# Transposes of a ternary feed-forward moved from TensorE to DMA, with the row rounding moved to ScalarE

## What is computed

```python
def _quant_weight(w):
    scale = jnp.mean(jnp.abs(w)) + EPS
    wq = jnp.clip(jnp.round(w / scale), -1.0, 1.0) * scale
    return w + jax.lax.stop_gradient(wq - w)

def _quant_act(x):
    scale = jnp.maximum(jnp.max(jnp.abs(x), axis=-1, keepdims=True), EPS) / 127.0
    xq = jnp.clip(jnp.round(x / scale), -128.0, 127.0) * scale
    return x + jax.lax.stop_gradient(xq - x)

def bitlinear(x, w):
    return jnp.einsum('bsi,oi->bso', _quant_act(x), _quant_weight(w))

gate = jax.nn.sigmoid(bitlinear(x, w_gate))      # 512 -> 2048
up = bitlinear(x, w_up)                          # 512 -> 2048
h = gate * up
return bitlinear(h, w_down)                      # 2048 -> 512
...
x = x + jnp.tanh(g_ffn[0]) * _L0_ffn_ref(_layernorm(x, axis=-1), L0_ffn_w_gate, L0_ffn_w_up, L0_ffn_w_down)
```

## Time and profile before

| | us |
|---|---|
| median of 3 runs | 1309.91 (1309.18 to 1309.97) |
| the profiled execution, its own time | 1311.82 |
| its span in the trace | 1310.0 |
| busy in the span: TensorE matmul | 1114.2 (85%) |
| VectorE | 1020.2 (78%) |
| ScalarE | 668.9 (51%) |
| GpSimd | 525.9 (40%) |
| all 16 DMA engines, mean share | about 31% |

### The profile page before, as it was taken

The page is one execution under the profiler, slowest core; times in us unless marked ns, Lnnn a source line. Parts: engine busy times, 40 slices in busy tenths (PEclk is TensorE's granted clock), DMA queues, the critical chain, the costliest instruction groups (busy, mean ns, idle before and its releaser), DMA issues. The chain is left out here.

```text
span 1310.0 us, 16066 instructions
## 1 busy us (share of the span) xinstructions
PE 1114.2 (85%) x4802; PEld 449.6 (34%) x4802; DVE 1020.2 (78%) x1560; ACT 668.9 (51%) x783; POOL 525.9 (40%) x403
## 2 busy tenths in 40 slices
PE   4976499999899899937999995999999998279687
PEld 2543022222222222203444442444444444134232
DVE  5677498887788788517999983688788878777888
ACT  1646047887688688844666663011000000586896
POOL 5756011535343353450101111888888784000021
PEclk9989569999899899978999997899999999589879
DMA  8799624436345354214111101111112110000011
GB/s 319 254 315 337 200 84 142 132 124 192 107 128 158 112 155 122 72 32 188 34 47 48 48 17 36 34 63 65 60 53 65 63 50 31 1 1 1 1 64 65
DMA packets 65213, 131.65 MB, mean 100 GB/s; under 512 B 13864, under 2 KB 31656, under 8 KB 61552
## 3 DMA queue, kind: packets, MB, share of 16 engines
q1 hardware_dynamic: 65152, 130.95, 30.7%
HBM read 106.53 MB, written 22.02 MB: 98 GB/s over the span
## 5 line engine op out<-in xcount | busy, mean ns | idle before, releaser
L807 DVE TENSOR_REDUCE mneg<-ps_m 128x1 f32<-128x512 f32 x512 | 319.6, 682 | 67.5 <-PE ps_m L720 55.7
L1348 PE MATMUL ps_y<-kv,toeplitz_sb 128*128 128x512 f32 x640 | 279.5, 596 | 8.6 <-POOL kv L1260 8.6
L688 ACT ACTIVATE probs<-ps_s 128x1024 f32<-128x1024 f32 x256 | 251.3, 1022 | 66.0 <-PE ps_s L742 65.0
L720 PE MATMUL ps_m<-k_stack,q_stack 112*128 112x512 bf16 x512 | 189.3, 410 | 26.9 <-DMA k_stack<-mask_k 16.1
L1348 PEld LDWEIGHTS ps_y<-kv,toeplitz_sb 128*128 128x128 f32 x640 | 121.1, 191 | 154.8 <-issue 154.8
L742 PE MATMUL ps_s<-q_stack,k_stack 112*128 112x512 bf16 x512 | 155.2, 387 | 10.4 <-ACT probs L688 10.1
L752 PE MATMUL ps_o<-probs,v_all 128*17 128x512 f32 x1024 | 136.5, 605 | 0.4 <-ACT probs L688 0.4
L1260 POOL TENSOR_TENSOR kv<-vT,ctxT_sb 128x2048 f32<-128x2048 f32 x32 | 118.8, 3711 | 39.2 <-PE ps_y L1348 32.4
L983 PE MATMUL ps_g<-w,xT_f 128*128 128x512 bf16 x512 | 119.7, 383 | 7.1 <-DVE h_f L1130 6.3
L1414 DVE TENSOR_TENSOR z<-ps_y,ctxT_sb 128x1024 f32<-128x1024 f32 x64 | 77.9, 1218 | 47.2 <-PE ps_y L1348 47.2
L1313 ACT ACTIVATE w_anchor<-w_f 128x512 f32<-128x512 f32 x32 | 20.1, 628 | 180.6 <-DMA w_f<-in_w 180.6
(11 more groups left out here) (159 smaller groups left out, 1628.1 us busy)
## 6 DMA issues: line engine op xcount, KB each, us to landing
w_sweep<-in_w SPq DMA_DIRECT2D x8, 1536.0 KB, 10.1
q_stack<-q_parts SPq DMA_DIRECT2D x96, 128.0 KB, 3.5
k_stack<-k_parts SPq DMA_DIRECT2D x96, 128.0 KB, 3.3
w_sweep<-in_w SPq DMA_DIRECT2D x16, 768.0 KB, 5.4
w_sweep<-in_w SPq DMA_DIRECT2D x16, 512.0 KB, 3.4
toeplitz_sb<-in_toeplitz SPq DMA_DIRECT2D x32, 256.0 KB, 2.6
w_f<-in_w SPq DMA_DIRECT2D x32, 256.0 KB, 2.9
k_parts<-qk_part SPq DMA_DIRECT2D x24, 256.0 KB, 6.9
```

Source lines behind the costliest of these rows:

```text
L688: nc.scalar.activation(pr[:, k % 2, 2 * slot:2 * slot + 2, :], S[:, 2 * slot:2 * slot + 2, :], ACT.Exp).then_inc(exp_done, 1)
L720: nc.tensor.matmul(M[:, bank(j), :], Q[0:ROWS, slot, hd, tc * P:(tc + 1) * P], K[0:ROWS, slot, hd, :], start=True, stop=True).then_inc(max ...
L807: nc.vector.tensor_reduce(mneg[:, h, tile % LT, tile // LT:tile // LT + 1], M[:, bank(j), :], AX.X, ALU.max, negate=True).then_inc(max_red, 1)
L1348: mm = nc.tensor.matmul(Y[:, q % 3, l2, :], T[:, g % 2, (lt - m) * P:(lt - m + 1) * P], kv[:, g % 2, m, :], start=(m == 0), stop=(m == lt))
```

## The change

The transposes leave TensorE: SyncE issues one DMA from SBUF to SBUF with `transpose=True` for each `xq_f` tile (128x512, 128 KB) and one for each `hq_f` tile (128x2048, 512 KB). The copies out of PSUM go with them. Centring and both rounding steps of the rows go from VectorE to ScalarE, as `centre` and `round_x`; for that one small operation (`nb`, 128x16) is added before the first tile. The maximum, the scales and the reciprocal stay in VectorE's `prepare`. The tile loop is written out in full. The `ctxT_sb` loads move behind the first tile's `turn_x(1)` in SyncE's queue. GpSimd's update of tile t-2 is written in the pass of tile t.

```diff
 def over_tiles(eng, n, tile):
 
-    tile(0, 0, True, False)
-    tile(1, 1, False, False)
-    with eng.Fori(1, n // 2 - 1) as i:
-        tile(2 * i, 0, False, False)
-        tile(2 * i + 1, 1, False, False)
-    tile(n - 2, 0, False, False)
-    tile(n - 1, 1, False, True)
+    for t in range(n):
+        tile(t, t % 2, t == 0, t == n - 1)
...
             @block.sync
             def _(sp):
+                def turn_x(t, par):
+
+                    sp.wait_ge(xq_ready, t + 1)
+                    if t >= 2:
+                        sp.wait_ge(gu_done, NCH * (t - 1))
+                    sp.dma_start(xT[:, par], xq[:, par, :], transpose=True).then_inc(xT_ready[par], 16)
+
+                def turn_h(t, par):
+
+                    sp.wait_ge(hq_ready, t + 1)
+                    if t >= 2:
+                        sp.wait_ge(down_done, t - 1)
+                    sp.dma_start(hT[:, par], hq[:, par, :], transpose=True).then_inc(hT_ready[par], 16)
+
                 def tile(t, par, first, last):
                     if not early(t):
                         sp.wait_ge(w8m_ready, t - 1)
                     sp.dma_start(w8c[:, par], A["w8"][bass.ds(2 * t, 2)].rearrange("m p l -> p m l"))\
                         .then_inc(w8c_loaded[par], 16)
-
-                for lt in range(LT):
-                    sp.dma_start(core.cT[:, lt], A["ctxT"][lt * P:(lt + 1) * P]).then_inc(core.cT_loaded, 16)
+                    if not last:
+                        turn_x(t + 1, 1 - par)
+                    if not first:
+                        turn_h(t - 1, 1 - par)
+                    if first:
+                        for lt in range(LT):
+                            sp.dma_start(core.cT[:, lt], A["ctxT"][lt * P:(lt + 1) * P]).then_inc(core.cT_loaded, 16)
+                    if last:
+                        turn_h(t, par)
+
+                turn_x(0, 0)
                 over_tiles(sp, ROWT, tile)
...
                 def down(t, par, first):
                     if not first:
                         pe.wait_ge(d_taken, t)
-                    for half in range(2):
-                        pe.wait_ge(hT_ready, 2 * t + half + 1)
-                        for k in range(half * KT // 2, (half + 1) * KT // 2):
-                            mm = nc.tensor.matmul(D[:], hT[:, par, k, :], wd[:, k, :], start=(k == 0),
-                                                  stop=(k == KT - 1))
+                    pe.wait_ge(hT_ready[par], 16 * (t // 2 + 1))
+                    for k in range(KT):
+                        mm = nc.tensor.matmul(D[:], hT[:, par, k, :], wd[:, k, :], start=(k == 0), stop=(k == KT - 1))
                     mm.then_inc(down_done, 1)
...
                         if c == 1 and not early(t):
                             down(t - 2, par, same(t, 2))
-                        if c == 2 and not last:
-                            turn_x(t + 1, 1 - par)
-                        if c == 3 and not first:
-                            turn_h(t - 1, 1 - par, same(t, 1))
...
             @block.scalar
             def _(act):
                 ln_scalar(core, act, 1)
...
+                act.wait_ge(xf_start, 1)
+
+                def centre(t, par):
+
+                    nc.scalar.activation(xn[:, par, :], X[:, t, :], ACT.Identity, bias=nb[:, t:t + 1],
+                                         scale=core.rstd[:, t:t + 1]).then_inc(xn_ready, 1)
+
+                def round_x(t, par):
+
+                    act.wait_ge(rx_ready, t + 1)
+                    nc.scalar.activation(xn[:, par, :], xn[:, par, :], ACT.Identity, bias=core.magic,
+                                         scale=sc[:, par, RX:RX + 1]).then_inc(xr_ready, 1)
+                    act.wait_ge(xr_ready, t + 1)
+                    if t >= 2:
+                        act.wait_ge(xT_ready[par], 16 * (t // 2))
+                    nc.scalar.activation(xq[:, par, :], xn[:, par, :], ACT.Copy, bias=-MAGIC).then_inc(xq_ready, 1)
+
+                centre(0, 0)
+                centre(1, 1)
+                round_x(0, 0)
...
                         nc.scalar.activation(sg[:, c % 2, :], G[:, c % 2, 0, :], ACT.Sigmoid,
                                              scale=sc[:, par, GS:GS + 1]).then_inc(sig_ready, 1)
+                        if c == 0 and not last:
+                            round_x(t + 1, 1 - par)
                         if c == 1 and not first:
                             round_h(t - 1, 1 - par)
-                        if c == 2 and not last:
-                            copy_x(t + 1, 1 - par, first)
+                        if c == 3 and t + 2 < ROWT:
+                            centre(t + 2, par)
                         if c == 2 and not early(t):
                             take_down(t - 2, par, same(t, 2))
-                        if c == 3 and not first:
-                            copy_h(t - 1, 1 - par)
...
-                    step(nc.vector.tensor_scalar(xn[:, par:par + 1, :], X[:, bass.ds(t, 1), :],
-                                                 core.mean[:, bass.ds(t, 1)], core.rstd[:, bass.ds(t, 1)],
-                                                 ALU.subtract, ALU.mult))
+                        dve.wait_ge(x_step, 3 * n + steps[0])
+
+                    dve.wait_ge(xn_ready, t + 1)
                     step(nc.vector.tensor_reduce(col(par, AMAX), xn[:, par, :], AX.X, ALU.max,
                                                  apply_absolute_value=True))
                     step(nc.vector.tensor_scalar(col(par, SX), col(par, AMAX), QEPS, 1.0 / 127.0, ALU.max, ALU.mult))
-                    step(nc.vector.reciprocal(col(par, RX), col(par, SX)))
-                    step(nc.vector.tensor_scalar(xn[:, par, :], xn[:, par, :], col(par, RX), MAGIC, ALU.mult, ALU.add))
+                    nc.vector.reciprocal(col(par, RX), col(par, SX)).then_inc(rx_ready, 1)
                     step(nc.vector.tensor_scalar(sc[:, par, GS:US + 1], core.w_scale[:, 0:2], col(par, SX), None,
                                                  ALU.mult))
-                    nc.vector.tensor_scalar(xq[:, par, :], xn[:, par, :], -MAGIC, None, ALU.add)\
-                        .then_inc(xq_ready, 1)
```

## The result

The changed kernel takes 1336.95 us (median of 4 runs, 1336.02 to 1338.44) beside 1309.94 us of the kernel before on the same chip: 1.020 times as long, 95% interval 1.0184 to 1.0215. The profiled execution has a span of 1334.2 us.

The account below looks back on a forecast made before the run. VectorE bounds the 12.06 us pass; ScalarE's new queue order makes it 13.65. Middle +22.4, loads +1.0, start +2.1 and end +7.2 give +32.7 us, 1342 us after rounding, range 1328 to 1410.

Parts of the forecast that it names:

- Who sets the pass: Steady part before the change: VectorE sets the 12.06 us pass, and TensorE has about half a microsecond to spare.
- The order of ScalarE's queue: Steady pass: sigmoids 1 and 2 queue behind rounding steps, VectorE idles 3.05 us against 1.44 saved, pass 13.65 us.
- The transposes: DMA landings taken as 6.5 us for `hq_f` and 3.0 for `xq_f`, both hidden in the steady pass.
- What they may take for nothing: Landing time free in the steady pass: 8.4 us for `hq_f`, about 7.3 for `xq_f`.
- Start: Stage start, deviation's reciprocal to first matmul: row steps on ScalarE, then 3.0 us for the DMA, +2.1 us.
- End: Stage end after product 0 of tile 15: +0.9 before `round_h(15)`, +4.6 for landing, +1.7 for last `down`, together +7.2 us.
- Middle: Product 0 of tile 0 to that of tile 15: 179.92 us becomes 202.35, +22.4; queued 1 MB loads add 1.0.
- Sum: Whole kernel: 22.4 + 1.0 + 2.1 + 7.2 = +32.7 us, rounded to 1342 us.
- The prediction's own case of a 3.4 us landing: Whole kernel if the inner transpose lands in 3.4 us: 1335 us, with the stage's end at +1.6.
- a landing of 9.7: Whole kernel at the slow transpose bound: 14 passes at +0.65 and 9 more at the end, put at 1370 us.
- (15 + 18.84) / 2: Rival of landings of 10 to 20 us: at 15 the pass is 17.0, about 1405 us; chance 15%.
- TensorE's clock: Rival: TensorE's clock falls to 1.2 GHz for its new pauses, 10.38 doubles to 20.8, about 1450 us; chance 5%.

Follow-up runs that it names:

- the kernel with two spares: Changed kernel with two spare transposes of the same 512 KB tile ahead of the real one in SyncE's queue; 1347.32 us in its one run.
- the kernel with four spares: Changed kernel with four spare transposes of the same 512 KB tile ahead of the real one in SyncE's queue; 1404.98 us in its one run.
- the six kernels: Changed kernel with ScalarE reordered (1327.49, 1313.77 us); DMA transposes without the row move (1314.78); row work split between VectorE and ScalarE, three versions (1310.73, 1308.25, 1307.40).

## Why the prediction was right, point by point

- *Who sets the pass.* VectorE, by its gapless timeline: confirmed twice. Taking 1.13 us off TensorE alone left the pass at 12.03; taking 0.92 off VectorE, with the queue of ScalarE in good order, brought 11.48, where TensorE takes over.
- *The order of ScalarE's queue.* Forecast 13.65, measured 13.59; product 1 at 3.79, measured 3.85; product 2 at 6.19, measured 6.16. The two waits were put at 1.85 and 1.2 and are 2.06 and 1.02: the first was counted from an end of `prepare` at 1.95, which is at 667.38 - 665.59 = 1.79. Undoing the order in two steps gave 13.02 and 11.44, against 13.06 and 11.4, and the order alone, without DMA transposes, gave 13.59, so this cause is shown.
- *The transposes.* Hidden, as forecast. The sizes taken, 6.5 and 3.0 us, were too dear: they are 3.6 and 2.3. The plain 512 KB load's 3.4 was the nearer row and not the middle of the two bounds.
- *What they may take for nothing.* Forecast 8.4. The landing of the kernel with two spares, 8.0 counted to the start of `down`, was hidden with 0.1 us to spare, 11.9 was not: about 8.1 is the bound.
- *Start.* +2.1 forecast, +2.13 measured to product 0, but that this is so close is luck. The forecast was for the first matmul, and there it is 593.28 - 586.77 = 6.51 against 593.98 - 589.24 = 4.74, +1.77: the landing was put too dear by some 0.5 and the steps before it 0.2 too cheap. The other 0.36 comes in tile 0's first matmuls, for which the working had nothing.
- *End.* +7.2 forecast, +2.04 measured. This is the mis-sized term, and it is the landing time again: the text's own figure for a landing of 3.4 was +1.6. Part by part (rows of the end, above): `round_h(15)` comes 11.22 after product 0 and not 11.86, since it waits for VectorE and not for `take_down(14)`: -0.64 where +0.9 was forecast. From its end to the last `down` it is 818.43 - 814.64 = 3.79 in place of 1.87: +1.92, not +4.6. That `down` takes 5.61 in place of 5.20, not 6.9, although TensorE stood 7.43 us before it: +0.41, not +1.7. Behind it 0.35 more are lost, which nothing foresaw.
- *Middle.* +22.4 and 1.0 for the loads forecast, +22.62 measured. The steady passes were each 0.06 cheaper than forecast; the pass of tile 0 was 1.0 dearer (12.85, not 11.85), the one for the loads not seen. That the middle comes out within 1 us is these errors cancelling.
- *Sum.* +32.7 forecast, +26.8 in the stage. The difference is the end's 5.2 and the loads' 1.0, less small change. The prediction's own case of a 3.4 us landing, 1335, was the better one.
- *Slips of the working.* At a landing of 9.7 its terms, 14 x 0.65 and 9 more at the end, give about 1361 and not 1370, and (15 + 18.84) / 2 is 16.9 and not 17.0. Neither touches the forecast.
- *TensorE's clock.* It stayed at 1.00 through the steady part, as was held against that rival. It did fall at the edges: 0.57 from 604 to 608, in tile 0's pass.
- *The Trainium skill's two rules.* A 512 KB transpose lands in 3.6 us. From 674 to 680 of the kernel with four spares, when nothing but transposes moves, the DMA engines carry 263 GB/s at full share (second row of that stretch, above). The effective 261 GB/s of the Trainium skill ("DMA: Bandwidth & Descriptors", latency and other measured facts), given there for a non-contiguous middle dimension, agrees; its 350 to 400 for the contiguous case was not reached here. The sum that the prediction drew from it, some 5 us smaller, would have been near 1337.6, an estimate, and 1336.95 was measured. The 1309 ns for one 128x128 of the Trainium skill ("VectorE: DVE Perf Modes", the three transpose paths) doesn't add up block by block: 16 blocks land in 3.6 us, and a pass takes 13.59 and not 26.2.

## What to carry to other kernels

Moving work to an engine with idle time pays only if its new place in that engine's queue doesn't put a short, early step behind a wait. Write out who is queued behind each new wait, and follow one pass with starts and ends: here totals said 10.6 us, the order said 13.65, and the chip said 13.59. When an order is mended, mend it up to the next consumer, or the wait only moves on (2.06 became 2.47). And a transfer that is hidden in the steady part is still paid in full where nothing covers it, at the stage's start and end.

## What the runs showed of the hardware that I had not expected

- A transposing DMA from SBUF to SBUF of 512 KB lands in 3.6 us, nearly as fast as the plain 512 KB load of this stage (3.4 in the kernel before, 3.7 in the changed one); one of 128 KB lands in 2.3. Its issue holds SyncE's queue 1.2 us (128 KB) or 1.6 (512 KB), and 1.9 to 2.3 for 512 KB once several are under way.
- A 512 KB load issued behind 4 MB of others kept VectorE waiting 3.73 us, and a 128 KB transpose after them landed 7.6 us after its issue. With the 4 MB elsewhere the first wait went and the second landing took 5.0, still over the usual 2.3. It landed in 4.8 to 7.6 in the six kernels where the stage's first inner transpose followed it by 1.2 to 1.8 us; the cause is open.
- After 6.31 us without work TensorE ran 16 matmuls in 6.29 us (3.62 at full clock), with the granted clock at 0.50 from 668 to 672, where pauses of under 2 us in every pass of the changed kernel left the clock at 1.00.
